# Routing in eight groups during attention, with rows scattered into first- and second-choice tables

## The reference, cut to what matters

```python
# x: (4, 1024, 256), ctx: (4, 77, 256); 16 heads of 16
x = x + xattn(layernorm(x), ctx)            # softmax(q k^T / 4) v, projections with biases
n = layernorm(x).reshape(4096, 256)         # the rows that are routed
scores = softmax(n @ wg)                    # 8 experts
gates, idx = top_k(scores, 2)
gates = gates / clip(sum(gates), EPS)
masks = one_hot(idx, 8)                     # (4096, 2, 8)
counts = masks.sum(0)
offsets = concat([zeros(1, 8), cumsum(counts)[:-1]])   # second choices stand behind all first ones
loc = cumsum(masks, 0) - 1 + offsets        # place of a token at its expert
keep = loc_sel < C                          # C = 1280
h = silu(disp @ fc1_w + fc1_b)              # (8, 1280, 1024)
y = h @ fc2_w + fc2_b                       # (8, 1280, 256)
combined = sum(gates * y[pos])
res = n + combined
out = x + layernorm(res) * gamma + beta
```

## Time and profile before

| what | value |
|---|---|
| median of three executions | 826.8 us (825.55 to 829.11) |
| the profiled execution | 823.38 us |
| its span | 821.6 us |
| mean granted TensorE clock | 0.911 of full speed |
| TensorE busy | 690.6 us (84%) |
| VectorE busy | 578.2 us (70%) |
| ScalarE busy | 396.3 us (48%) |
| GpSimd busy | 439.7 us (54%) |

### The profile page before, as it was taken

How to read it: one execution, slowest core, us unless ns; L and a number is a source line. 1 busy time by engine, 2 the same in 40 slices (tenths; PEclk the granted TensorE clock), 3 DMA queues, 4 the chain that set the end, 5 groups by cost and what they waited for, 6 DMA issues and landing times.

```text
span 821.6 us, 16511 instructions
## 1 busy us (share of the span) xinstructions
PE 690.6 (84%) x5636; PEld 655.8 (80%) x5637; DVE 578.2 (70%) x1174; ACT 396.3 (48%) x901; POOL 439.7 (54%) x483
## 2 busy tenths in 40 slices
PE   4799999999999313799999996999969999999500
PEld 3589999999998202799999996999969999999500
DVE  4699898988886798366556676677657565764178
ACT  2355555555555312345444464455445444653174
POOL 5746546546452346724455556657537555532466
PEclk9799999999999655699999997999989999999855
DMA  9401011111111240313443545345443443322374
GB/s 280 148 26 40 27 40 40 34 34 40 40 40 40 78 108 0 93 32 75 104 95 49 100 104 106 62 99 108 102 96 53 105 98 54 53 34 27 39 237 172
DMA packets 55334, 63.91 MB, mean 78 GB/s; under 512 B 9296, under 2 KB 50512, under 8 KB 55120
## 3 DMA queue, kind: packets, MB, share of 16 engines
q0 software_dynamic: 15360, 21.31, 15.9%
q1 hardware_dynamic: 34784, 40.96, 15.4%
q10 hardware_dynamic: 5104, 0.44, 0.5%
HBM read 38.96 MB, written 23.72 MB: 76 GB/s over the span
## 4 chain that ended last, share of the span: by engine, by line
PE 78%; DVE 10%; issue 4%; DMA 3%; POOL 2%; ACT 1%; SPq 0%; DVEq 0%; POOLq 0%; ACTq 0%
PE banks L776 18%; PE banks L778 17%; PE banks L777 17%; PE banks L889 8%; PE banks L875 5%; PE banks L863 5%; PE banks L997 2%; PE banks L947 2%; POOL oh_id L549 2%; DMA sum_rows<-y_sb,slot_ids 1%; DVE z L1454 1%; DMA wq_sb<-in_wqT 1%; PE banks L902 1%; PE banks L937 1%; PE banks L806 1%
## 5 line engine op out<-in xcount | busy, mean ns | idle before, releaser
L527 POOL DMA_INDIRECT sum_rows<-y_sb,slot_ids x80 | 129.7, 1621 | 189.8 <-ACT y_sb L725 165.0
L735 ACT ACTIVATE hraw<-banks,b_now 128x256 f32<-128x256 f32 x320 | 132.6, 475 | 107.4 <-PE banks L778 98.8
L776 PE MATMUL banks<-xT_hi,w_hi 128*128 128x256 f32 x560 | 164.0, 293 | 5.8 <-issue 3.4
L778 PE MATMUL banks<-xT_hi,w_lo 128*128 128x256 f32 x560 | 160.7, 287 | 0.0
L777 PE MATMUL banks<-xT_lo,w_hi 128*128 128x256 f32 x560 | 160.6, 287 | 0.0
L776 PE MATMUL banks<-w_hi,h_hi 128*128 128x256 f32 x528 | 149.0, 282 | 2.7 <-issue 2.7
L777 PE MATMUL banks<-w_lo,h_hi 128*128 128x256 f32 x528 | 148.6, 281 | 0.0
L778 PE MATMUL banks<-w_hi,h_lo 128*128 128x256 f32 x528 | 148.5, 281 | 0.0
L1398 DVE CAST h_hi<-hraw 128x512 fp32r<-128x512 f32 x160 | 73.0, 456 | 67.9 <-ACT hraw L735 66.1
L1400 DVE TENSOR_TENSOR h_lo<-hraw,h_hi 128x512 fp32r<-128x512 f32 x160 | 113.5, 709 | 5.5
L776 PEld LDWEIGHTS banks<-xT_hi,w_hi 128*128 128x128 f32 x560 | 109.0, 195 | 6.4 <-issue 6.4
(11 more groups left out here) (194 smaller groups left out, 1458.0 us busy)
## 6 DMA issues: line engine op xcount, KB each, us to landing
w1raw<-in_w1T SPq DMA_DIRECT2D x8, 1024.0 KB
w2raw<-in_w SPq DMA_DIRECT2D x8, 1024.0 KB
xn_rows<-xn SPq DMA_DIRECT2D x32, 128.0 KB, 1.7
sum_rows<-xn SPq DMA_DIRECT2D x32, 128.0 KB, 1.8
out<-z SPq DMA_DIRECT2D x16, 256.0 KB, 2.2
res<-sum_rows SPq DMA_DIRECT2D x7, 512.0 KB, 7.4
X<-in_x SPq DMA_DIRECT2D x2, 1280.0 KB, 13.8
xg<-xn_rows,slot_ids POOLq DMA_INDIRECT x80
```

The source lines that it names most:

```text
L527: g.indirect_dma_start(sum_rows, bass.IndirectOffsetOnAxis(ap=slot_ids[:, st, 1, q:q + 1], axis=0), y_sb[:, u, q, :], None, bounds_check=N ...
L735: a.activation(hraw[:, j // 2, j % 2, :], banks[:, j // 2, (j % 2) * 256:(j % 2 + 1) * 256], ACT.Silu, bias=b1_now[:, (c // SPE) % 2, j:j ...
L776: t_.matmul(o, a_hi, b_hi, start=first, stop=False)
L778: return t_.matmul(o, a_lo, b_hi, start=False, stop=last)
```

## The change

Tokens are routed in eight groups of tiles: 6, 6, 6, 6, 3, 2, 2 and 1. A group is chosen in the step in which its last tile's logits are made; TensorE counts it (`count`), VectorE turns the count into a row number per choice. Choosing is 11 small VectorE operations (six functions pick_a to pick_f of two and, the last, one), summing up two, and placing (place_a, place_b: a product and a sum) and gating (gate_a, gate_b) four more; for the first four groups these last four come in the next step. In a step with scatters the first tile's first scatter stands first on POOL, the rest last. When the groups are done, four VectorE operations make the list of first-choice rows, and more the list of second ones, and then the first expert's four w_lo. For the last four groups all of this is in one step. The row number of a choice is 8 times its place among the choices of its expert plus the expert. POOL writes normalised row, gates and the token's own number into a ring of twelve tiles and scatters each tile twice, by first choice into first_rows and by second choice into second_rows, from step 10 on. Both tables are filled with zeros at the start, and 512 rows behind the second hold the numbers of spare rows. The experts gather each half of a super-tile from the first table and then from the second; numbers out of bounds are passed over. The scatter takes its row numbers from the gathered rows. xn_rows and the one-hot inversion are gone. VectorE takes the first expert's low parts and the additions of beta from POOL, and makes the last three tiles' normalised rows.

```diff
-    xn_rows = nc.dram_tensor("xn_rows", [N, W], f32, kind="Internal").ap()
+    first_rows = nc.dram_tensor("first_rows", [NE * CAP, W], f32, kind="Internal").ap()
+    second_rows = nc.dram_tensor("second_rows", [EMPTY_ROWS + 4 * P, W], f32, kind="Internal").ap()
...
+        GROUPS = [(0, 6), (6, 12), (12, 18), (18, 24), (24, 27), (27, 29), (29, 31), (31, 32)]
+        NGRP = len(GROUPS)
+        AT_ONCE = NGRP - 4
+        ROWS_BY_DVE = NT - 3
...
+            if 10 <= t <= 27:
+                return range(t - 10, t - 9)
+            return {28: range(18, 20), 29: range(20, 21), 30: range(21, 23), 31: range(23, 25), 32: range(25, 27),
+                    33: range(27, 29), 35: range(29, NT)}.get(t, range(0))
...
+            for r in range(NR):
+                wait(engine, row_out[r][t % 2], 16 * ((t - ROW_RING) // 2 + 1))
+            wait(engine, sum_out[t % 4], 16 * ((t - ROW_RING) // 4 + 1))
...
+            sp.wait_ge(sem("empty_made"), 1)
+            for rows in (first_rows, second_rows):
+                sp.dma_start(rows[0:NE * CAP, :].rearrange("(p n f) w -> p n (f w)", p=P, f=4),
+                             row_ring[:, 8:12, :].rearrange("p f w -> p (f w)").unsqueeze(1)
+                             .to_broadcast([P, NE * CAP // P // 4, 4 * W])).then_inc(tables_zeroed, 16)
+            sp.dma_start(second_rows[EMPTY_ROWS:EMPTY_ROWS + 4 * P, :].rearrange("(q p) w -> p q w", p=P),
+                         row_ring[:, 4:8, :]).then_inc(sem("empty_stored"), 16)
...
+                t = 2 * i + u - 3
+                if within(t, NT):
+                    sp.wait_ge(sem("xn2_made"), t + 1)
+                    wait(sp, sum_out[t % 4], 16 * (t // 4))
+                    sp.dma_start(sum_rows[t * P:(t + 1) * P, :], ring_row(t)[:, 0:D]).then_inc(sum_out[t % 4], 16)
...
+            g.memset(row_ring[:, 4:12, :], 0.0).then_inc(sem("cleared"), 1)
+            pool.wait_ge(sem("cleared"), 8)
...
+                for a in tiles_to_scatter(t)[:1]:
+                    scatter_rows(a, 0)
...
+                    ring_free(pool, t - 2)
+                    if t - 2 == 4:
+                        pool.wait_ge(sem("empty_stored"), 16)
+                    if t - 2 == 8:
+                        pool.wait_ge(tables_zeroed, 32)
+                    if t - 2 < ROWS_BY_DVE:
+                        centre(ring_row(t - 2)[:, 0:D], t - 2, mv2[:, u, 0:1], "xn2_centred")
+                        pool.wait_ge(sem("rstd2_made"), t - 1)
+                        pool.wait_ge(sem("xn2_centred"), t - 1)
+                        scale(ring_row(t - 2)[:, 0:D], rstd2[:, u:u + 1], "xn2_made")
+                    g.iota(ring_row(t - 2)[:, IDC:W].bitcast(i32), pattern=[[0, W - IDC]], base=(t - 2) * P,
+                           channel_multiplier=1).then_inc(sem("ids_written"), 1)
...
+                for n, a in enumerate(tiles_to_scatter(t)):
+                    if n:
+                        scatter_rows(a, 0)
+                    scatter_rows(a, 1)
+            gated = [0]
+            def scatter_rows(t, r):
+                k = group_of_tile(t)
+                if t == 0:
+                    pool.wait_ge(tables_zeroed, 32)
+                if k >= gated[0]:
+                    a, b = GROUPS[k]
+                    pool.wait_ge(sem("e_scaled"), k + 1)
+                    ring = slice(a % ROW_RING, a % ROW_RING + b - a)
+                    g.tensor_tensor(row_ring[:, ring, D:IDC], e_all[:, a:b, :],
+                                    e_scale[:, a:b].unsqueeze(2).to_broadcast([P, b - a, NE]), ALU.mult)\
+                        .then_inc(sem("gated"), 1)
+                    gated[0] = k + 1
+                if r == 0:
+                    pool.wait_ge(sem("gated"), k + 1)
+                    pool.wait_ge(sem("ids_written"), t + 1)
+                    pool.wait_ge(sem("xn2_made"), t + 1)
+                    pool.wait_ge(sem("row_no_made"), k + 1)
+                wait(pool, row_out[r][(t - 1) % 2], 16 * ((t - 1) // 2 + 1))
+                g.indirect_dma_start((first_rows, second_rows)[r],
+                                     bass.IndirectOffsetOnAxis(ap=row_no[:, t, r:r + 1], axis=0),
+                                     ring_row(t), None, bounds_check=NE * CAP - 1, oob_is_err=False)\
+                    .then_inc(row_out[r][t % 2], 16)
...
+            def gather_second(st):
+                if within(st, NST):
+                    u = st % SPE
+                    pool.wait_ge(gathered_first[u], 32 * (st // SPE + 1))
+                    for q in range(2):
+                        g.indirect_dma_start(xg[:, st % XR, q, :], None, second_rows,
+                                             bass.IndirectOffsetOnAxis(ap=slot_second[:, st, q:q + 1], axis=0),
+                                             bounds_check=EMPTY_ROWS + 4 * P - 1, oob_is_err=False).then_inc(gathered[u], 16)
...
+            for n in range(2):
+                pool.wait_ge(row_out[0][n], 16 * NT // 2)
+            gather_first(0)
+            gather_first(1)
+            pool.wait_ge(sem("ids_made"), 2)
+            for n in range(2):
+                pool.wait_ge(row_out[1][n], 16 * NT // 2)
             for n in range(4):
+                pool.wait_ge(sum_out[n], 16 * NT // 4)
+            pool.wait_ge(sem("empty_stored"), 16)
+            gather_second(0)
+            pool.wait_ge(sem("trash_zeroed"), 16)
+            for st in range(2, AHEAD + 1):
+                gather_first(st)
+                gather_second(st - 1)
+            for st in range(NST + 2):
+                gather_first(st + AHEAD + 1)
+                gather_second(st + AHEAD)
+                scatter(st - 2)
             pool.wait_ge(load_gb, 32)
...
+                if t == NT + 1:
+                    split_quarter(0, 0, 0)
+                    split_quarter(0, 0, 1)
...
+                def count(k):
+                    a, b = GROUPS[k]
...
+                    at = banks[:, CB, 0:RE * (b - a)].rearrange("p (t c) -> p t c", c=RE)
...
+                    t_.matmul(at, eights[:], of_tile(run[:, k, :], b - a), start=True, stop=False)
+                    for j in range(b - a):
+                        mine = sel[:, a + j].rearrange("p r e -> p (r e)")
+                        if j < b - a - 1:
+                            t_.matmul(at[:, j + 1:, :], eights[:], of_tile(mine, b - a - 1 - j), start=False, stop=False)
+                        m = t_.matmul(at[:, j, :], upper[:], mine, start=False, stop=(j == b - a - 1))
+                    m.then_inc(sem("counted"), 1)
...
+                if group_of_step(t) is not None:
+                    count(group_of_step(t))
                 weigh_values(3)
...
+            def pick_a(k):
+                a, b = GROUPS[k]
+                dve.wait_ge(sem("logits_made"), b)
+                routed(v.tensor_reduce(top[:, a:b], logits[:, a:b, :], AX, ALU.max))
+                last()
+                v.tensor_tensor(below[:, a:b, :], logits[:, a:b, :], over_e(top[:, a:b], b - a), ALU.subtract)\
+                    .then_inc(sem("router_shifted"), 1)
+            def pick_b(k):
+                a, b = GROUPS[k]
...
+                routed(v.scalar_tensor_tensor(weigh[:, a:b, :], below[:, a:b, :], 0.0,
+                                              first_of[:].unsqueeze(1).to_broadcast([P, b - a, NE]),
+                                              ALU.is_equal, ALU.mult))
+                last()
+                routed(v.tensor_reduce(tpick[:, a:b], weigh[:, a:b, :], AX, ALU.max))
...
+            def add_up(k):
+                a, b = GROUPS[k]
+                dve.wait_ge(sem("sel_made"), k + 1)
+                wait(dve, sem("run_made"), k)
...
+                routed(v.tensor_reduce(taken[:], sel[:, a:b].rearrange("p t r e -> p (r e) t"), AX, ALU.add))
+                last()
+                v.tensor_tensor(run[:, k + 1, :], run[:, k, :], taken[:], ALU.add).then_inc(sem("run_made"), 1)
...
+                    if t - 2 >= ROWS_BY_DVE:
+                        dve.wait_ge(sem("rstd2_made"), t - 1)
+                        ring_free(dve, t - 2)
+                        v.tensor_scalar(ring_row(t - 2)[:, 0:D], xt, mv2[:, u, 0:1], rstd2[:, u:u + 1],
+                                        ALU.subtract, ALU.mult).then_inc(sem("xn2_made"), 1)
+                if picked is not None and picked < AT_ONCE:
+                    add_up(picked)
+                if picked is not None and picked >= AT_ONCE:
+                    place_a(picked)
+                    place_b(picked)
+                    add_up(picked)
+                    gate_a(picked)
+                    gate_b(picked)
...
+            dve.wait_ge(sem("counted"), NGRP + 1)
+            end_first, end_second = banks[:, CB, TOTALS:TOTALS + NE], banks[:, CB, TOTALS + NE:TOTALS + RE]
...
+            for n in range(4):
+                dve.wait_ge(sem("w_hi_made"), n + 1)
+                hi, lo, raw = w_parts(0, n)
```

(4 more changed lines are left out.)

454 lines of the change are left out of this document (225 added, 229 removed).

## The result

The changed kernel takes 843.3 us in the median of four runs (837.8 to 849.3), beside 826.2 for the kernel before (four runs, 825.4 to 829.1): a ratio of 1.020, 95% interval 1.012 to 1.028. It is slower; 816 had been forecast, and the range ended at 837. The profiled execution took 845.05 us with a span of 843.3.

A forecast was written before the change was run, and what follows sets the result against it. TensorE was taken as full in attention and experts, with a 57.2 us VectorE chain between. Gap -28.4, large groups +12, groups 5 and 6 +2.5 and +1.5, fill +1.5: -10.9, so 816 us; range 805 to 825, with rivals 799 to 837.

The forecast's parts named there:

- The group term: Attention: choosing, counting and placing delay TensorE 3.0 us per large group, 12 for four; bounds 1.5 and 5 each.
- The slack: Attention, one pair of steps: 0.2 us before values, 0.75 before X's logits; VectorE idles 1.15 us in the odd step.
- The collisions: Attention: eight two-input VectorE operations per group wait for POOL's, about 0.15 us each, 1.2 in all, half inside idle time.
- The end of attention: Steps 30 and 32: group 5 costs 2.5 us and group 6 1.5 us.
- Rival C: Attention and last rounds: POOL becomes the bound, 16.1 us needed of 15.0 per pair of steps; 834 us, chance 0.13.
- The gap: Last logits' copy to first expert matmul: shrinks from 57.2 to 28.8 us, a gain of 28.4.
- the landing of a scatter: Last scatter rounds before the expert stage: each lands about 3.5 us after it may start, read from a gather pair.
- The fill: Start: 22.8 MB of table stores end at 77.7 to 86.6 us and cost 1.5 us, bounds 0 and 4.5.
- Rival B: Start: the fill holds POOL in step 6, ending at 103.8 us, 21.7 late; 836 us, chance 0.15.
- The expert stage: Experts: POOL at 9.4 us per super-tile of 10.8 keeps pace; change 0, between -2 and +6 us.
- rival D: Expert stage: TensorE passes super-tiles without tokens quickly and POOL, at 9.4 us each, falls behind; 822 us, chance 0.12.

The follow-up runs named there:

- kernel 7: The changed kernel with the key rows put back ahead of q_lo, nothing else different; 833.8 us, ratio 1.009.
- kernel 3: The kernel before plus 17 small VectorE choice operations per large group, key rows ahead of q_lo, no count, no scatter; 841.8 us, ratio 1.019.
- kernel 5: The changed kernel without the scatters of tiles 0 to 23; 852.9 us, ratio 1.033.
- kernel 1: The kernel before with only q_lo moved ahead of the key rows in VectorE's odd steps; 836.5 us, ratio 1.011.
- experiment 4: The kernel before with the three stores of the tables' fill (22.8 MB) behind the last load of X; 848.7 us, ratio 1.027.
- kernel 16: The changed kernel with key rows ahead of q_lo and moved off steps 9 and 15, b2 and expert 1 loads held, POOL's gathers paced; 826.9 us, ratio 1.001.

## Why the prediction was wrong

**The group term is the step that failed.** The prediction takes 3.0 us per large group, 12 for four, with bounds of 1.5 and 5 for each; it was 6.6, 9.2, 3.9 and 5.5, 25.2 in all. The sum adds up delays of TensorE and has no term for the clock behind them. From the values of step 9 to those of step 30, the changed kernel and then the one before:

```profile
100.29:283.81 183.52, 172.20 (x1421) 156.20 (x1418) 155.40 (x391) 92.28 (x229) 127.31 (x201) 0.93 0.14 47
92.68:251.05 158.37, 158.37 (x1373) 145.03 (x1370) 137.14 (x322) 90.69 (x221) 84.83 (x137) 1.00 0.11 36
```

TensorE's waits there in the changed kernel (us in total, times, longest):

```profile
PE banks L1043 <- DVE X L1438: 11.3, 6, 3.4
```

TensorE idles 11.3 us in this stretch, in six waits, all for X, and its granted clock of 0.93 takes some 13 us more. So the stalls came out close to the 12 forecast, and the lower clock, put at nothing, is the larger half of the cost. That the stalls come so near is partly luck: by group they are 3.2, 4.3, 1.9 and 1.9 us, and two of the six waits, 0.9 us each, are of steps 11 and 17, where the swapped key rows are made and nothing is chosen. In kernel 7 the four groups cost 24.4, with 9.4 us of stalls.

Two smaller things in the working were off. The slack was read off one pair of steps from 206 us on the earlier trace rows, in which no key rows are made, and taken for all; in kernel 3 the groups of steps 9 and 15 cost 5.3 and 5.0 us, those of steps 21 and 27 2.9 and 1.1. And the choice is not all of a group: VectorE's operations alone made 14.3 of the 24.4 us that kernel 7 pays. The other 10 (the count on TensorE, and the work beside POOL's scatters) weren't taken apart; the 2.8 us that kernel 5 saves are within the spread of single traces. The collisions were there, but small (one `weigh` of 0.50 us, where the reduction behind it takes 0.20).

**A line of the diff was not costed at all:** q_lo ahead of the key rows. Alone it makes the kernel before 10 us slower, and putting it back makes the changed one 9.5 us faster. Of the 7.6 us by which step 9 is late, 3.1 are added behind step 3 and are this, before any routing (6.3 in kernel 1); the 4.5 that step 3 is late by stand before the first swapped operation and lie in the scatter of the start.

**The end of attention** was given 4 us for groups 5 and 6 and took 6.7. Rival C is half right: in steps 24 to 27 scatters run and the lateness stays at 27.3, so POOL is not the bound there at 1.0 to 1.2 us per scatter. From step 30, with two tiles a step, it has a part: VectorE waits 2.4 us for POOL's 1/sigma and 0.7 for a scatter's landing, and TensorE 3.4 us for the values behind them.

**The gap** was forecast as 28.8 and came out at 34.0, inside the bound of 5.7. The term that was mis-sized is the landing of a scatter, taken as 3.5 us a round from a row of gathers with quiet queues: loads of 3 MB run beside it here. With these held back the rounds are 3.3 to 3.6 us and the gap 27.8, so the rest of the working stands. By the formula of the Trainium skill (DMA: Bandwidth & Descriptors, Anatomy of one DMA) the gap would be an estimated 24.8; no run came there.

**The fill** did no visible harm: its last store landed at 78.0 us, near the early end of the forecast 77.7 to 86.6, and POOL didn't wait for it. Whether it cost the 1.5 us can't be told from the scatter of the start. It moved 406 to 420 GB/s, above the 405 that the prediction took as its upper bound. Rival B's mechanism, POOL standing for a buffer behind the fill, is what experiment 4 shows on the kernel before, with 21 us; the change's longer ring keeps it away.

**The expert stage** was put at 0, between -2 and +6, and is 5.2 us longer: rival D in small. TensorE's waits there, after and before:

```profile
PE banks L1083 <- issue: 14.7, 5, 8.5
PE banks L850 <- issue: 2.7, 3, 1.2
```

```profile
PE banks L997 <- issue: 6.5, 5, 3.7
PE banks L776 <- issue: 6.1, 4, 3.4
```

The longest, 8.5 for 3.7 us, stands where an expert's last super-tiles have no tokens: TensorE passes them, and POOL, with six DMAs per super-tile instead of four and nothing but 0.3 us between them, hasn't gathered the next rows yet.

## What to carry to other kernels

Where one engine is full at full clock, an added wait costs its length and, in most of the cases here, some us at half clock behind it, so price a stall by a stretch of the trace behind a like stall, and look for slack in each step that an edit touches, not in one that stands for all. Read a diff for what it reorders, not only for what it adds; a swap of two short operations was worth 10 us here. And when the work on a shared queue grows, break up long series of transfers and keep bulk loads out of a stretch in which short transfers wait for each other.

## What the runs showed of the hardware that I had not expected

- A TensorE wait of 0.8 us was followed by about six us at the lower clock level (rows of experiment 1); the pair of 1.05 and 0.66 us by four or more. Not every wait was: in kernel 16 one of 1.3 us for X, between 97 and 145 us, left the granted clock at 1.00.
- TensorE issued single matmuls 0.7 to 1.4 us apart for some 13 us behind its entry into the expert stage, in six kernels, and in neither of the two in which POOL's gathers were paced (86 matmuls in ten us instead of 16).
- Stores of zeros to memory ran at 420 GB/s from 40 to 60 us and at 406 to 80, while operations of VectorE and ACT beside them kept their durations (the maxima of the scores 793 ns against 792, the exponentials 712 against 713).
